# Values and turns in pairs and a ring of three banks in a decoder's attention; one output job a unit later

## The reference

```python
def _L1_xattn_ref(trg, enc, mask, sa_w, sa_b, ca_w, ca_b, ln_g, ln_b, w1, b1, w2, b2):
    L, D, H, FF = (6, 256, 16, 1024)
    ...
    def mha(xq, xkv, W, B, mask):
        ...
        q = proj(xq, W[0], B[0])
        k = proj(xkv, W[1], B[1])
        v = proj(xkv, W[2], B[2])
        score = jnp.einsum('bhqd,bhkd->bhqk', q, k) / math.sqrt(DH)
        if mask is not None:
            score = jnp.where(mask[:, None] == 0, -10000.0, score)
        attn = jax.nn.softmax(score, axis=-1)
        out = jnp.einsum('bhqk,bhkd->bhqd', attn, v)
        out = out.transpose(0, 2, 1, 3).reshape(bsz, -1, D)
        return out @ W[3] + B[3]

    def step(x, p):
        saw, sab, caw, cab, lg, lb, W1, B1, W2, B2 = p
        h = mha(x, x, saw, sab, mask)
        x = layer_norm(h + x, lg[0], lb[0])
        h = mha(x, enc, caw, cab, None)
        x = layer_norm(h + x, lg[1], lb[1])
        h = jax.nn.relu(x @ W1 + B1) @ W2 + B2
        x = layer_norm(h + x, lg[2], lb[2])
        return (x, None)
```

```python
def _L3_xattn_ref(x, y, Wq, bq, Wkv, bkv, q_gamma, q_beta, k_gamma, k_beta, Wproj, bproj):
    ...
    q = _layernorm(q, q_gamma, q_beta) * SCALE
    k = _layernorm(k, k_gamma, k_beta)
    attn = jax.nn.softmax(jnp.einsum('bhnd,bhmd->bhnm', q, k), axis=-1)
    out = jnp.einsum('bhnm,bhmd->bhnd', attn, v)
    out = out.transpose(0, 2, 1, 3).reshape(B, N, C)
    return out @ Wproj.T + bproj
```

## The kernel before

| unit | jobs before, in order |
| --- | --- |
| 0 | K0, V0, K1, V1, S0 (two transposes, L2063) |
| 1 | n (two transposes, L2063), S1q (L2070, VectorE L2209), K2, S1k (L2070), K3 |
| 2 | q (L2070), K4, Y (L2092, VectorE L2184) |
| 3 | S3 (L2102, VectorE L2217), K5, V2, K6 |
| 4 | D0 (two transposes, L2063, ScalarE L2327), V3, V4, V5 |
| 5 | S2 (L2096, VectorE L2215), D1 (L2122), K7, V6 |
| 6 | S6 (L2110, VectorE L2221), D2, V7, and once a layer X |
| 7 | S7 (L2115), D3 (L2127) |

## Time and profile before

### The profile page before, as it was taken

One profiled execution on the slowest core, in us unless ns is written; L12 is line 12 of the kernel. 1 busy time (PEld: TensorE's weight loads), 2 busy tenths in 40 slices (PEclk: granted clock), 3 DMA queues, 4 the chain that ended last, 5 costly groups with the idle time before them and its releaser, 6 DMA issues. The chain is left out here.

```text
span 4821.1 us, 104294 instructions
## 1 busy us (share of the span) xinstructions
PE 4121.2 (85%) x43410; PEld 3131.6 (65%) x43410; DVE 2635.7 (55%) x5604; ACT 1862.3 (39%) x5080; POOL 301.6 (6%) x562
## 2 busy tenths in 40 slices
PE   6987993999999999999999997669588777777767
PEld 4765882777777777777777775458355577555535
DVE  2435112677777777777777764721367545244445
ACT  1221220444444444444444443212266444254423
POOL 0000101000000000000000000010211000000000
PEclk9998896999999999999999998769799788888878
DMA  3110483001101101111111100048445200100000
GB/s 126 66 59 3 147 302 105 28 32 43 45 32 43 54 26 46 49 31 41 49 40 32 48 28 9 2 160 305 143 146 160 75 0 0 32 27 19 10 1 11
DMA packets 116918, 310.49 MB, mean 64 GB/s; under 512 B 29352, under 2 KB 75625, under 8 KB 92017
## 3 DMA queue, kind: packets, MB, share of 16 engines
q1 hardware_dynamic: 113392, 295.61, 18.0%
q0 software_dynamic: 3072, 8.39, 0.5%
HBM read 289.01 MB, written 14.94 MB: 63 GB/s over the span
## 5 line engine op out<-in xcount | busy, mean ns | idle before, releaser
L2353 ACT ACTIVATE layers_probs<-banks,layers_negmax 128x257 f32<-128x257 f32 x768 | 357.6, 471 | 998.3 <-DVE layers_negmax L2233 998.3
L2077 PE MATMUL banks<-ctx_tiles,weights_a 128*128 128x257 f32 x1536 | 407.2, 388 | 25.3 <-ACT layers_nT L2327 25.3
L2083 PE MATMUL banks<-weights_a,ctx_tiles 128*128 128x256 f32 x1536 | 379.4, 380 | 0.0
L2077 PEld LDWEIGHTS banks<-ctx_tiles,weights_a 128*128 128x128 f32 x1536 | 271.0, 191 | 79.1 <-ACT layers_nT L2327 33.7
L2083 PEld LDWEIGHTS banks<-weights_a,ctx_tiles 128*128 128x128 f32 x1536 | 285.3, 191 | 35.1
L2233 DVE TENSOR_REDUCE layers_negmax<-banks 128x2 f32<-128x514 f32 x384 | 262.3, 683 | 71.0 <-PE banks L2138 71.0
L2213 DVE TENSOR_TENSOR layers_V<-banks,rows_a 128x256 f32<-128x256 f32 x384 | 160.3, 418 | 192.9 <-PE banks L2083 187.0
L2138 PE MATMUL banks<-layers_KT,layers_qblk 32*64 32x257 f32 x3072 | 256.0, 403 | 10.7 <-ACT layers_probs L2353 8.2
L2146 PEld LDWEIGHTS banks<-const,layers_probs 128*128 128x128 f32 x1536 | 162.0, 141 | 149.2 <-issue 149.1
L2146 PE MATMUL banks<-const,layers_probs 128*128 128x128 f32 x1536 | 253.3, 288 | 0.0
L2358 ACT COPY layers_pT<-banks 128x512 f32<-128x512 f32 x384 | 223.6, 582 | 3.3 <-PE banks L2146 3.3
(11 more groups left out here) (704 smaller groups left out, 8384.2 us busy)
## 6 DMA issues: line engine op xcount, KB each, us to landing
ctx_tiles<-in_ctx SPq DMA_DIRECT2D x65, 1028.0 KB, 5.0
weights_a<-in_L_w SPq DMA_DIRECT2D x44, 1024.0 KB, 5.1
l2x_B<-positions SPq DMA_DIRECT2D x32, 1280.0 KB, 5.9
weights_b<-in_L_w SPq DMA_DIRECT2D x32, 1024.0 KB, 6.4
weights_c<-in_L_w SPq DMA_DIRECT2D x16, 1024.0 KB, 7.0
weights_b<-in_L_xattn_w SPq DMA_DIRECT2D x12, 1024.0 KB, 7.4
l0x_key_rows<-in_ctx_rows SPq DMA_DIRECT2D x32, 256.0 KB, 2.6
ctx_tiles<-in_ctx_keys SPq DMA_DIRECT2D x32, 256.0 KB, 2.7
```

Source lines behind the costliest of these rows:

```text
L2077: last = mm(o[:, 0:LK], ca_wk[:, c, m * P:(m + 1) * P], E.ctx[:, tile % 2, c, j * LK:(j + 1) * LK], start=c == 0, stop=c == DC - 1)
L2083: last = mm(o[:, 0:D], E.ctx[:, tile % 2, c, first:first + P], ca_wv[:, c], start=c == 0, stop=c == DC - 1)
L2353: a(probs[:, cc, j, t], ps[:, t, 0:LK], ACT.Exp, bias=negmax[:, k % 2, t:t + 1], accum_out=totals[:, cc, t, j:j + 1]).then_inc(s["exp_done ...
```

## The change

In `decoder_layers`:
- Turns and values are done for two units at a time: in even units the turns of `it - 2` and `it - 1`, in odd units the values of `it - 3` and `it - 2`. ScalarE's two copies follow in the even units.
- The turns get two banks (2 and 3) by turns and wait for the copy of two units before; the values' bank is 4, and the ring has the three banks that are left (5 to 7), RB = 3.
- n is the last job of unit 1 instead of the first.

In `context_attention` the output job Y is placed in unit 4 instead of unit 3.

```diff
@@ -607,7 +607,7 @@
     jobs, at, by_unit = [], {}, {}
     for it in its:
         placed = []
-        if it >= U and it % U == LAG:
+        if it >= U and it % U == LAG + 1:
             placed.append((it // U - 1, "Y", None, "dve"))
         if it // U + 1 < NG:
             placed += [(it // U + 1, *job) for job in prep[starts[it % U]:starts[it % U + 1]]]
@@ -1874,7 +1874,7 @@
     KC = 2
     VC = GB * KC
     U = DC * GB
-    TURN, PV, RING, RB = 2, 3, 4, 4
+    TURN, PV, RING, RB = 2, 4, 5, 3
 
     def k_job(i):
         return ("K", (i // GB, i % GB), "act")
@@ -1884,7 +1884,7 @@
 
     UNIT_JOBS = [
         [k_job(0), v_job(0), k_job(1), v_job(1), ("S0", None, "act")],
-        [("n", None, "act"), ("S1q", None, "dve"), k_job(2), ("S1k", None, "act"), k_job(3)],
+        [("S1q", None, "dve"), k_job(2), ("S1k", None, "act"), k_job(3), ("n", None, "act")],
         [("q", None, "act"), k_job(4), ("Y", None, "dve")],
         [("S3", None, "dve"), k_job(5), v_job(2), k_job(6)],
         [("D0", None, "act"), v_job(3), v_job(4), v_job(5)],
@@ -2140,10 +2140,10 @@
 
                 def transposes(k, pos, cc, j):
                     need(pe, "exp_done", 2 * (k + 1))
-                    need(pe, "copied", k)
+                    need(pe, "copied", k - 1)
                     for t in range(2):
                         for c in range(KC):
-                            last = tr(ps[:, TURN, (KC * t + c) * P:(KC * t + c + 1) * P], probs[:, cc, j, t, 1 + c * P:1 + (c + 1) * P], E.c("ident"))
+                            last = tr(ps[:, TURN + k % 2, (KC * t + c) * P:(KC * t + c + 1) * P], probs[:, cc, j, t, 1 + c * P:1 + (c + 1) * P], E.c("ident"))
                     last.then_inc(s["transposed"], 1)
 
                 def values(k, pos, cc, j):
@@ -2166,11 +2166,13 @@
                 for it in range(N * U):
                     if ca_unit(it):
                         scores(*ca_unit(it))
-                    if ca_unit(it - 1):
+                    if it % 2 == 0 and ca_unit(it - 1):
+                        transposes(*ca_unit(it - 2))
                         transposes(*ca_unit(it - 1))
                     for a in jobs_in(it):
                         job(*a)
-                    if ca_unit(it - 2):
+                    if it % 2 and ca_unit(it - 2):
+                        values(*ca_unit(it - 3))
                         values(*ca_unit(it - 2))
 
             @blk.vector
@@ -2355,13 +2357,14 @@
                 def copy_transposed(k, pos, cc, j):
                     act.wait_ge(s["transposed"], k + 1)
                     need(act, "pv_done", k - 1)
-                    nc.scalar.copy(pT[:, k % 2].rearrange("p t c x -> p (t c x)"), ps[:, TURN]).then_inc(s["copied"], 1)
+                    nc.scalar.copy(pT[:, k % 2].rearrange("p t c x -> p (t c x)"), ps[:, TURN + k % 2]).then_inc(s["copied"], 1)
 
                 for it in range(N * U):
                     step, u = it // U, it % U
                     if ca_unit(it):
                         exponentials(*ca_unit(it))
-                    if ca_unit(it - 1):
+                    if it % 2 == 0 and ca_unit(it - 1):
+                        copy_transposed(*ca_unit(it - 2))
                         copy_transposed(*ca_unit(it - 1))
                     for b in jobs_in(it):
                         take(*b)
```

## The result

| | median us | runs, us | decoder stretch, us | last cross attention, us | a full decoder step, us |
|---|---|---|---|---|---|
| before | 4820.74 | 4 runs, 4812.34 to 4822.97 | 2172.6 | 416.1 | 43.69 |
| after | 5132.35 | 4 runs, 5129.9 to 5138.77 | 2500.2 | 397.7 | 48.60, then 51.22 |

After against before is 1.0652, interval 1.0633 to 1.067: slower by 311.6 us, where 200 were forecast. The direction was right, the time is 47 us above the upper end of the range. The profiled execution after took 5130.44 us, its span 5128.3. The stretches of the table are those of the two profiled executions, which lie 307 us apart. All of the growth is the decoder's (+327.6); the last cross attention is shorter by 18.4, the rest of the program by 2.1.

The account below looks back on a forecast made before the run. TensorE's own work bounds the decoder; new waits of 6.31 us a step, less 0.70 and 0.85 saved, give +214 over 45 steps; with -14 from the last cross attention, 4823.2 becomes 5023 (5019 on the median's footing), range 4961 to 5085.

Parts of the forecast that it names:

- K(3) for S1q: Decoder unit 1: key job K(3) waits for VectorE's evacuation of S1q, three jobs ahead; 2.30 us a step, 2.41 with start-up.
- K(6) for S3, with S3's own wait: Decoder unit 3: K(6) waits 1.89 us a step for S3's evacuation; S3's possible wait counted at nothing.
- V(6) for S2: Decoder unit 5: value job V(6) waits for VectorE's evacuation of S2; 1.48 us a step, 1.59 with start-up.
- V(5) for D0, with its start-up: Decoder unit 4: V(5) waits for ScalarE's copy of D0; 0.31 us a step, the wait between 0 and 0.8.
- start-up behind a wait: TensorE in the decoder: the record behind a wait runs longer than an unwaited one, by 0.11 us.
- two units of values: TensorE in the decoder: two units' values in a row take 0.58 us start to start, where one took 0.36.
- first job of an odd unit behind scores: Decoder odd units: the first job behind the scores pays 0.05 us for the change of tile shape.
- the savings: TensorE in the decoder: pairing turns and values means fewer changes of tile shape, saving 0.70 us a step.
- the third rival: Decoder: only K(3)'s wait costs time, the later waits vanish; 4844 us; chance 0.07, shared with another part of the waits.
- the second: Rival for the decoder: the three-bank ring costs nothing and only savings stand; 4735 us, chance 0.03.
- the clock's rival: Decoder: the new waits also lower TensorE's granted clock, 92 us on top, 5111 us; chance 0.07 for falling throughout.
- The last cross attention: With Y one unit later, key jobs fill its wait for attnT; -14 us, between 0 and -43.

Follow-up runs that it names:

- e5: The changed kernel with eight unread identity matmuls ahead of K(3) alone, filling that wait; 5027.06 us, ratio 1.0432 to the kernel before.
- e7: The kernel before with only its decoder job table re-ordered; four-bank ring, single turns and values kept; 4777.45 us, ratio 0.9908.
- e6: The changed kernel with its decoder jobs in another order, keeping the three-bank ring, pairs and later Y; 4736.68 us, ratio 0.9828 to the kernel before.
- e9: The changed kernel with one unread identity matmul ahead of K(3) alone, shortening that wait; 5129.28 us, ratio 1.0644 to the kernel before.
- e3: The kernel before with only Y of the last cross attention moved one unit later; 4793.82 us, ratio 0.9953.
- e1: The kernel before with only the decoder's ring cut from four banks to three; 4969.91 us, ratio 1.0318.

## Why the prediction was wrong

**What held.** The mechanism and its sizes at full clock. A step became 48.60 us long, +4.91; forecast was +4.76. The kernel with these waits and without the falling clock, e5, takes 5027 us, where the sum was 5019. By its terms, measured start to start as the forecast did, less the job's own time (0.89 for S1k, 0.87 for V(2) and K(7)):

| term, us a step | forecast | shown | where |
|---|---|---|---|
| K(3) for S1q | 2.30 | 2.30 | after: 1402.92 to 1406.11 is 3.19, less 0.89 |
| K(6) for S3, with S3's own wait | 1.89 | 1.94 | e5: 1405.38 to 1408.05 is 2.67, less 0.87, and S3's 0.14 |
| V(6) for S2 | 1.48 | 1.48 | after: 1430.62 to 1432.97 is 2.35, less 0.87 |
| V(5) for D0, with its start-up | 0.31 | 0.41 | three jobs of V in e5: 3.16 against 2.75 |
| start-up behind a wait | 0.11 | 0.10 | K at 1406.11 takes 1.13, at 1402.06 1.03 |
| two units of values | 0.58 | 0.58 | e5: 1409.12 to 1409.70 |
| first job of an odd unit behind scores | +0.05 | +0.08 to 0.11 | after: 1401.09 to 1402.06 (S1q) is 0.97, before 0.89; 1427.87 to 1428.84 (S2) is 0.97, before 0.86 |

The last row is the miss of the savings: with some 0.05 more in units 1, 5 and 7 (S3 in unit 3 pays nothing), the pairs save about 0.56 instead of 0.70. With D0's extra 0.10 and K(6)'s 0.05 the rows would make the step some 0.3 longer than forecast; it is 0.15 longer. Most of the difference is a small wait that the forecast overlooked and that the change takes away: ahead of the scores of unit 4, before, sixteen records of values take 0.48 where they take 0.36 elsewhere.

```profile
1791.32 0.43 PE L2158 MATMUL banks<-layers_pT,layers_V 128*32 128x64 f32 x16
1791.80 0.66 PE L2138 MATMUL banks<-layers_KT,layers_qblk 32*64 32x257 f32 x8
```

The expectation for e7 has it, 0.12 a step. S3's wait was counted at nothing, since it "shortens K(6)'s wait by as much"; so it did: 1.80 and 0.14 are the 1.89 within 0.05. The waits did add up and not hide one another, against the third rival; the ring of three was not free, against the second. Its point of decision (TensorE's work longer than the chain beside it) is right, though, and another order of the same jobs reaches it, at 4736.68 us, where the rival's price was 4735. That the two times are so close is luck, since e6 is another table. The rival named the condition and not the lever.

**What failed** is the step in which the clock's rival was weighed. In the sum the clock's term stood at nothing; it measured 98 us in the decoder. The rival's mechanism was there word for word ("new waits of 1.5 to 2.4 us, three a step, may do it as well"), with a size of 92 us; the chance was 0.07. That 92 is so near to 98 is partly luck: the rival has 90 falls at 1.02 us each, the trace has 74 at 1.3. The reason given against it was that the waits "are less than half of the idleness that did it there", 5.34 us in the earlier trace rows. That row shows that 5.34 us is enough; it doesn't show that less isn't, and the prediction had no row with an idleness of some 2 us and the clock's answer to it. The argument took the one case that the trace had for the edge. Runs then showed that 1.91 and 2.13 us are enough (e9, after) and 1.65 is not in any of 45 steps (e5). The section that the prediction named, in the Trainium skill's "TensorE: Matmul & The Clock Gate", "A second HAM failure mode: psum-queue depth-cycling", had said that cycling through banks can idle the engine often enough for the clock to swing: here it does, by the granted 0.50 behind K(3), and the prediction said itself that by this page the rival "would be likelier than I make it". The rival's own sum was 5111; with the decoder's measured 229 instead of 214 at full clock, 98 instead of 92 for the clock, -18 instead of -14 for the last cross attention and the -2 elsewhere it is 5126, against 5132 measured. The range stopped "a third of the way into the clock's case", which a chance of 0.07 allowed and an open question does not.

Why 2.6 us a step: the rival priced four slow records, as in the earlier trace rows. Behind K(3) the clock stays low through n, the values, the shares, the scores and half of the turns, and from K(3) to q it is 5.43 us where e5 has 3.97: 1.46 more. Behind K(6), up to D0, it is 1.56 more, but D0's wait of 0.41 is then gone: 1.15.

**The last cross attention.** Forecast -14, between 0 and -43. The stretch became 18.4 us shorter in after and 18.2 in e3, where the whole kernel was 24 faster (16 to 29). Y's waits for attnT are all but gone, and the key jobs fill the gap as forecast: ScalarE squares the keys with no idleness ahead, where the earlier trace rows has 2.25.

```profile
PE banks L703 <- DVE l3x_attnT L848: 1.9, 1, 1.9
PE banks L714 <- ACT l3x_probs L915: 33.1, 31, 1.7
...
4620.70 0.47 ACT L902 ACTIVATE l3x_sq<-banks,centred_bias 128x257 f32<-128x257 f32 x1
...
4621.59 1.13 PE L703 MATMUL banks<-weights_b,l3x_attnT 128*128 128x256 f32 x4
```

Y takes 1.13 in this row, where it took 2.05 in the earlier trace rows. The 32.8 us that Y's waits lost are not all gained. The scores' waits for the probabilities (L714) were 22.2 us in 27 waits before, 10.9 less than now. And the values (L735) now stand idle for 12.1 us in 7 times, where before has no such row; the profile gives no releaser for it, only "issue", and what these values wait for stays open:

```profile
PE banks L735 <- issue: 12.1, 7, 1.9
4619.25 0.43 PE L735 MATMUL banks<-l3x_pT,l3x_V 128*32 128x64 f32 x16 [1.92 <-issue]
```

**Still open.** What besides the length of the idleness decides whether the clock falls. In after it fell in one of the first five steps that have the 2.13 us, and in all 39 behind them, with the same 2.13 us each time. Open too is why K(6)'s wait is followed by a slow stretch only where K(3)'s was. K(6) idles 1.80 us in such a step and 1.65 in e5, so length may have a part in it; but in the steps from 1054.18 and 1201.50 it idles 1.80 as well, and the clock stays at 1.00 behind it. That K(3)'s wait sets it off is shown, by e5 against after; the rest is not.

## What to carry to other kernels

In a ring of n banks, a job waits for the evacuation of the job n places ahead of it: before a bank is given away, lay the chain of the engine that empties the banks beside the bound engine's work for every job, with the distance that will be left, and if one is short, move jobs before you look for banks; here the order alone was worth 396 us in a ring of three and 43 in a ring of four. Ask of each part of a paired change what it saves by itself: pairing the values gave 0.55 us a step and needed a third buffer for the turned probabilities, pairing the turns showed no gain and cost the bank. And a new wait of about 2 us on the bound engine, once in each pass of a loop, has a second price in the granted clock: it belongs in the range unless a row of the trace shows the same wait without it.

## What the hardware showed

One wait of 1.91 or 2.13 us in a step, in a stretch where TensorE is otherwise busy for some nine tenths of the time, can bring the clock down to 0.50 for about three microseconds, and not at once but 0.3 to 1.5 us behind the end of the wait; in 34 of 40 steps of after it fell a second time behind the next wait, of 1.80 us. The two falls together cost 2.6 us a step, more than the first wait itself, and 98 us in all. Filling that wait with matmuls whose results nobody reads makes the kernel faster by 105 us. The fall doesn't come with each such wait: in after one of the first five steps had it. From 1201.50 us on every step had it, and the steps with both falls then lasted 51.21 to 51.28 us, except at a change of layer. Waits of 1.65 us (e5) and of up to 1.5 us (e1) in every step did not bring it.
